# Causal attention in a four-layer decoder kernel: masked looks issued in pairs over four row groups, unmasked looks beside scores of the other row half

## The reference, cut to what matters

```python
def _L3_attn_ref(x, Wq, bq, Wk, bk, Wv, bv, Wo, bo, gamma, beta):
    ...
    q = split_heads(x @ Wq + bq)
    k = split_heads(x @ Wk + bk)
    v = split_heads(x @ Wv + bv)
    att = jnp.einsum('bhtd,bhsd->bhts', q, k) * (1.0 / math.sqrt(Dh))
    causal = jnp.tril(jnp.ones((T, T), dtype=bool))
    att = jnp.where(causal[None, None], att, -jnp.inf)
    att = jax.nn.softmax(att, axis=-1)
    o = jnp.einsum('bhts,bhsd->bhtd', att, v)
    o = o.transpose(0, 2, 1, 3).reshape(B, T, N_EMBD)
    y = o @ Wo + bo
    ...
```

## Time and profile before

| | us |
|---|---|
| median of 3 runs | 1919.76 |
| lowest, highest | 1915.0, 1927.36 |
| the profiled execution | 1901.9 |
| its span, first to last instruction | 1900.2 |
| the 64 units of weights in it, about | 1582 to 1768 |

### The profile page before, as it was taken

How to read it: one execution, slowest core, us unless ns; L and a number is a source line. 1 busy time by engine, 2 the same in 40 slices (tenths; PEclk the granted TensorE clock), 3 DMA queues, 4 the chain that set the end, 5 groups by cost and what they waited for, 6 DMA issues and landing times. The chain is left out here.

```text
span 1900.2 us, 50175 instructions
## 1 busy us (share of the span) xinstructions
PE 1677.1 (88%) x19970; PEld 1176.9 (62%) x19970; DVE 1127.5 (59%) x2410; ACT 973.6 (51%) x2317; POOL 706.7 (37%) x947
## 2 busy tenths in 40 slices
PE   6884899775799999999999878999999999999885
PEld 4332899343457888888888753567986655454332
DVE  4544445459657777787785433766658866563424
ACT  4552444458686666676664434334553253445552
POOL 1103311306256766766675301472016611223101
PEclk9997899796799999999999889899999999999998
DMA  7311686000041000000000040524643200000100
GB/s 297 135 42 53 204 243 206 26 1 1 1 155 38 26 15 25 15 15 25 15 25 15 26 200 1 126 84 118 170 131 80 63 1 1 2 2 1 41 1 24
DMA packets 75641, 125.69 MB, mean 66 GB/s; under 512 B 10696, under 2 KB 55120, under 8 KB 73776
## 3 DMA queue, kind: packets, MB, share of 16 engines
q1 hardware_dynamic: 67408, 106.69, 17.6%
q0 software_dynamic: 6912, 15.61, 2.7%
q10 hardware_dynamic: 1088, 0.13, 0.0%
HBM read 83.73 MB, written 38.67 MB: 64 GB/s over the span
## 5 line engine op out<-in xcount | busy, mean ns | idle before, releaser
L2908 DVE SCALAR_TENSOR_TENSOR big<-bank,pack,big 128x256 f32<-128x256 f32 (+2 forms) x384 | 182.8, 477 | 39.3 <-ACT mask L2797 23.5
L2796 ACT ACTIVATE big<-bank,pack 128x256 f32<-128x256 f32 x192 | 91.5, 477 | 128.1 <-PE bank L2604 123.7
L3336 ACT ACTIVATE pt<-bank 128x1024 f32<-128x1024 f32 (+3 forms) x128 | 84.2, 704 | 105.7 <-PE bank L3182 105.5
L3366 DVE TENSOR_REDUCE part<-bank 128x8 f32<-128x1024 f32 (+1 forms) x80 | 95.6, 1220 | 68.2 <-PE bank L3163 68.2
L2129 ACT ACTIVATE pack<-bank 128x512 f32<-128x512 f32 x96 | 57.6, 600 | 152.6 <-PE bank L785 120.6
L2514 POOL TENSOR_TENSOR big<-big,mask 128x256 f32<-128x256 f32 (+1 forms) x128 | 93.8, 733 | 88.6 <-DVE big L2908 54.8
L2604 PE MATMUL bank<-y,pack 128*128 128x262 f32 (+1 forms) x384 | 120.9, 400 | 4.2 <-DVE big L2908 4.0
L2591 PE MATMUL bank<-big 128*128 128x128 f32 x896 | 123.1, 284 | 1.1 <-issue 1.1
L1927 POOL DMA_INDIRECT pack<-results,where x64 | 67.5, 1055 | 150.5 <-PE bank L1998 139.2
L783 PE MATMUL bank<-yh,wl 128*128 128x512 f32 x192 | 112.6, 586 | 7.1 <-DVE a L2289 5.4
L3105 POOL TENSOR_SCALAR_AFFINE_SELECT pt<-pt 128x256 f32<-128x256 f32 x128 | 54.1, 427 | 156.8 <-ACT pt L3336 156.4
(11 more groups left out here) (664 smaller groups left out, 4421.5 us busy)
## 6 DMA issues: line engine op xcount, KB each, us to landing
big<-in_experts SPq DMA_DIRECT2D x46, 516.0 KB, 4.4
big<-in_big SPq DMA_DIRECT2D x1, 9216.0 KB, 25.8
gate<-big SPq DMA_DIRECT2D x32, 256.0 KB
z<-gate SPq DMA_DIRECT2D x16, 512.0 KB, 3.5
pack<-routing SPq DMA_DIRECT2D x60, 128.0 KB, 3.0
wide_sorted<-big SPq DMA_DIRECT2D x5, 1472.0 KB, 13.1
pack<-in_pack SPq DMA_DIRECT2D x1, 5910.5 KB, 21.2
pack<-wide_sorted SPq DMA_DIRECT2D x16, 256.0 KB, 3.1
```

What stands on the lines that cost most here:

```text
L2796: nc.scalar.activation(dst3(i), conv_in(i, 0), ACT.Copy, scale=weight(i, 3))
L2908: ins = nc.vector.scalar_tensor_tensor(out=d, in0=conv_in(i, back), scalar=weight(i, 3 - back), in1=d, op0=ALU.mult, op1=ALU.add)
L3336: nc.scalar.activation(dst, src, ACT.Exp, scale=-1.0).then_inc(s["weights"], 1)
L3366: nc.vector.tensor_reduce(dst, src, AX.X, ALU.max).then_inc(s["most"], 1)
```

## The change

Three things change. The two row halves of a look are listed in the other order (`gp` 1 first, then 0), so that in a unit the look behind W0 (rows 0 to 63) works on rows 64 to 127 and the look behind W1 on rows 0 to 63. The table `per_unit` always places looks two at a time and at other units. And where both looks of a unit are masked, the unit's order becomes W0, W1, then `look_masked`: the four mask matmuls of both looks, then their 16 score matmuls in turn over all four row groups; `ring` follows that order. The looks ahead of the units stay single. Counts of matmuls, exponentials and reductions stay the same. VectorE's and ScalarE's own order of work is the same but for the units at which reductions stand.

```diff
@@ -3039,10 +3039,10 @@
     looks = [(i, kind, key, w, js, gp) for i in range(TB) for kind, key, w in spans[i]
-             for js in (((1, 0, 3, 2),) if w == P else ((1, 0), (3, 2))) for gp in range(2)]
+             for js in (((1, 0, 3, 2),) if w == P else ((1, 0), (3, 2))) for gp in (1, 0)]
     LOOKS = len(looks)
 
-    per_unit = [(0, 1, 2, 2) * 3 + (0, 1, 0, 0)] + [(0, 2, 2, 2) + (0, 1, 2, 2) * 2 + (0, 2, 2, 0)] * 2
+    per_unit = [(0, 2, 2, 2) * 2 + (0, 0, 2, 0, 0, 0, 2, 0)] + [(0, 2, 2, 2) * 3 + (0, 0, 2, 0)] * 2
...
+    masked = lambda more: len(more) == 2 and looks[more[0] % LOOKS][1] == 0
     ring = [("most", at) for at in range(LOOKS + AHEAD)]
     for u in range(B * UNITS):
         more = list(looks_in(u))
-        ring += [("weights", 2 * u)] + [("most", at) for at in more[:-1]] + [("weights", 2 * u + 1)] + [("most", at) for at in more[-1:]]
+        if masked(more):
+            ring += [("weights", 2 * u), ("weights", 2 * u + 1)] + [("most", at) for at in more]
+        else:
+            ring += [("weights", 2 * u)] + [("most", at) for at in more[:-1]] + [("weights", 2 * u + 1)] + [("most", at) for at in more[-1:]]
...
+            def look_masked(first):
+                b, n = divmod(first, LOOKS)
+                i, kind, key, w, js, gp = looks[n]
+                for at in (first, first + 1):
+                    reuse(place["most", at])
+                    for gl in range(2):
+                        nc.tensor.matmul(both(place["most", at])[:, sl(gl)], k.ident_bf, later4[:, :], start=True, stop=False, skip_group_check=True)
+                for c, j in enumerate(js):
+                    for at in (first, first + 1):
+                        for gl in range(2):
+                            rows = sl(2 * looks[at % LOOKS][5] + gl, 32)
+                            mm = nc.tensor.matmul(both(place["most", at])[:, gl * S + c * w:][:, 0:w], qj[b][rows, j * S + i * P:][:, 0:P], kd[b][rows, key:key + w],
+                                                  start=False, stop=True, tile_position=(rows.start, 0), skip_group_check=True)
+                        if c == len(js) - 1:
+                            mm.then_inc(s["scores"], 1)
...
+                    more = looks_in(u)
                     weigh(u, 0)
-                    for at in looks_in(u)[:-1]:
-                        look(at)
+                    if not masked(more):
+                        for at in more[:-1]:
+                            look(at)
                     weigh(u, 1)
-                    for at in looks_in(u)[-1:]:
-                        look(at)
+                    if masked(more):
+                        look_masked(more[0])
+                    else:
+                        for at in more[-1:]:
+                            look(at)
```

## The result

Over 20 runs each, the changed kernel takes 1927.66 us (1916.29 to 1942.04) and the kernel before 1919.12 us (1911.29 to 1930.32): ratio 1.0044, with a 95% interval of 1.0024 to 1.0063. The interval is 4.6 to 12.1 us. The profiled execution took 1933.5 us, its span 1931.8.

A forecast was written before the change was run, and what follows sets the result against it. TensorE looked the bound, but its items wait in a ring of three slots for readers. Late start 0.37, batch 0 2.17, batches 1 and 2 -0.4 each: 1.7 us more on the median 1919.8, so 1921.5 us, range 1906 to 1932.

The forecast's parts named there:

- the ring of three slots: Looks and W0/W1 on TensorE: an item can't start before its slot's reader is done, 0.05 us behind the reader's end.
- their 1.4: Masked pairs on TensorE alone: each of 10 saves about 1.4 us if nothing waits, 14 us in all.
- Prices of units: Worked-out times of single units: unit 17 at 4.20, 18 at 4.37, 19 at 4.26, 14 at 4.19 us.
- the working: Unit by unit times from widths, the ring's order and durations; gave 54.63 us for the old batch 1, trace 54.72.
- The other row half: Looks beside W0 or W1 on the other row half: about nothing gained where widths are 256 or more.
- Four row groups overlap in pairs: Pair's 32 score records on TensorE: 1.00 + 0.10 us where two looks cost 2.18.
- The rival of no overlap: Four row groups don't overlap: each of 10 pairs takes 1.00 us more, 1931.5 us in all; chance 0.08.
- The saving stays: Rival: readers are done earlier, slots come free about 1 us sooner, pairs keep 1.4 us each, 1906 us; chance 0.12.
- The sum, 1.7 us: Whole change: 0.37 for unit 0's later start + 2.17 in batch 0 - 0.4 - 0.4 in batches 1 and 2.
- the dearest place: Unit 14 of batch 0: its second look needs W0's exponential, so 4.19 us instead of 1.19, 3.00 more.
- The forecast of 0.80: Chance 0.80 that the changed kernel takes between 1 us less and 5 us more than before.
- the bound of 56: Sign of being wrong: batch 1 clearly under 53 us (slots free earlier) or over 56 (pairs run half by half).

The follow-up runs named there:

- pairs_only: Kernel before with old table and old row halves, only the seven units whose two looks are both masked issued as pairs: 1909.00 against 1903.70 us, ratio 1.0027.
- no_pairs: Changed kernel with new table and new order of row halves, but each masked look single: 1920.37 us, ratio 1.0093 to the kernel before.
- r_after: Changed kernel run again with nothing altered, beside the kernel before: 1913.04 us, ratio 1.0039.
- halves_only: Kernel before with nothing changed but the order of row halves (gp 1, then 0): 1906.93 against 1904.56 us, ratio 1.0015.
- r_after2: Changed kernel run a third time, unaltered, in a later group on a second chip: 1917.81 us, ratio 1.0068 to the kernel before.

## Why the prediction was right and wrong, point by point

- **That the ring of three slots is tight, so pairs give back what they save**: right in the main. Batch 1 at full clock is 0.2 us shorter with 3.5 us less TensorE busy time, and `pairs_only` loses 0.6 us a batch. In the new table pairs do keep 0.5 us each of their 1.4, as `no_pairs` shows; the table's other places lose that again.
- **Prices of units**: right to 0.03 us for 17, 18, 19 and 14. In the profiles of all kernels without filling, the steps between units at full clock sum to within 1.0 us of the working (of some 180), and what they miss sits in units 11, 15, 27, 31 and 50, by 0.1 to 0.2 each. In batch 1, which the prediction shows in full, it is 54.49 against 54.20, with 0.10 in unit 27 and 0.22 in unit 31. Unit 0 starts 52.39 us behind the block's first matmul in `r_after`, 52.04 before: 0.35 later, where 0.37 were worked out. In all, the order costs 0.35 + 2.2 = 2.5 us at full clock, not 1.7.
- **The other row half is worth about nothing**: for single units of width 256, yes; as a change of the whole order it costs 0.93 us a batch in `halves_only`, which the unit by unit working contained and the sentence did not say.
- **Four row groups overlap in pairs**: right, 1.10 us for 32 records with their tail. The rival of no overlap fell.
- **The saving stays**: fell. The slots do not come free sooner.
- **The sum, 1.7 us**: the term that failed is one that was not in it. The working took the clock of 1.00 of the earlier trace rows as given for the changed order as well, so time at the lower clock stood at nothing without a reason. By the rule of 0.32 it was 4.6 us on one chip and 10.8 on another. Unit 14 was named as the dearest place and priced at 3.00 us for its wait, but the clock that falls behind this wait costs another 0.7 us in unit 14, 1.1 in unit 15 and 1.6 in unit 16 when it lasts that long. That is part of the term; what brings the rest of the falls stays open.
- **The forecast of 0.80, between 1 less and 5 more**: the median missed it. 8.5 us (4.6 to 12.1) lie between it and the rival of no overlap, and that rival is not the cause. The range took the result in because the rivals' prices made it wide, which is luck. No rival had the clock in it, and the signs of being wrong could not tell it from the others: batch 1 of `r_after2`, with 57.9 us, is over the bound of 56 without pairs running half by half.
- **Time from runs**: the added median of 1919.8 held (1919.1).

## What to carry to other kernels

When a change makes one engine faster, work out when each buffer it needs comes free; if two results land together, the reader needs twice its time before the second slot is back, and the gain goes there. Price a new wait on TensorE also by what stands behind it: a granted clock of 1.00 in the old order is no promise for the new one, and a few matmuls that nothing reads can test it. A table of placements is worth a unit by unit working: with one changed table the three batches are 6.6 us shorter at full clock, where the new instruction order made them 2 us longer.

## What the runs showed of the hardware

- Matmuls of different row groups run side by side: in the earlier trace rows W0's records start at 1611.22 and those of the other half's look at 1611.23. In a pair 32 score records over four row groups take 1.10 us to the values, as the 16 of a single look do over two (1.09).
- A reduction of 1.22 us behind another ends 1.14 us after it, and exponentials of 1.02 us start 0.91 us apart: durations overlap by 7 to 11%, and a working that adds them is too long.
- The time at the lower clock isn't fixed for a program: from 182 to 222 us in 28 runs of the same kernel on one chip, and each microsecond of it goes with 0.3 us of time. A single wait of 0.74 us more in a stretch that ran at a clock of 1.00 came with a fall in 7 of 9 places, and six unread matmuls a batch in its waits with none in 3.
